# Seventeen unread matrix products in three pauses of TensorE, in a six-stage convolution and attention kernel

## The chip, the core and the metric

The kernel runs on one core of one Trainium2 chip. The metric is the device time of one launch in microseconds (us), the median of several runs. The core's engines are TensorE (PE in the profile, its weight loads PEld), VectorE (DVE), ScalarE (ACT), GpSimd (POOL) and SyncE (SP, which here only issues DMAs). TensorE's clock has two levels, 1.2 and 2.4 GHz; the profile gives the granted clock as a share of the full one, so 0.50 is 1.2 GHz and 1.00 is 2.4 GHz.

## What is computed

Eight images of 64 channels and 16 x 16 pixels pass six residual layers, all in float32:

```python
x = x + _L0_conv_ref(_gn(x), ...)    # group norm, then a deformable 3x3 convolution
x = x + _L1_conv_ref(_gn(x), ...)    # group norm, 3x3 convolution mixed by gates and a 20-step Sinkhorn
t = _to_tokens(x)                    # 8 x 256 tokens of 64 channels
t = t + _L2_attn_ref(_ln_t(t), ...)  # causal attention, 8 heads
t = t + _L2_ffn_ref(_ln_t(t), ...)   # 8 experts, hidden 256, gelu, top 2
t = t + _L3_attn_ref(_ln_t(t), ...)  # windowed gated mean
t = t + _L3_ffn_ref(_ln_t(t), ...)   # 16 experts, hidden 128, silu gate, top 2
```

The three places that the change touches lie in the first group norm, in the Sinkhorn iteration of the second layer, and in the first layer norm ahead of the attention:

```python
def sinkhorn_knopp(H_tilde, t_max=20):
    M = jnp.exp(H_tilde)
    for _ in range(t_max):
        M = M / jnp.sum(M, axis=-1, keepdims=True)
        M = M / jnp.sum(M, axis=-2, keepdims=True)
    return M
```

## The kernel before, in words

Everything is written out by hand. Each engine has one program, executed in order, and the engines meet in counting semaphores: a producer counts one up, a consumer waits for a number. There is no scheduler, so the order in the text of an engine's program is its order on the chip. Channels lie on the partitions for the convolutions (two images side by side, 4 columns of image pairs, `J` = 4), tokens for the attention and the experts. PSUM is one tensor `PS` of 8 banks of 512 float32 columns, and each use names its bank.

TensorE's program in order, with the lines that matter here:

- **First group norm.** VectorE takes the moments of the input. TensorE averages them over pairs of channels by one small product (L1315, bank 7) and sends them back. VectorE and ScalarE make the normalised images (`G`, L798), split them and the offset weights into a high and a low part (`GHP`, L609; `WO`, L612 and L816; `GLP`, L811), and TensorE begins the offset convolution (L1324), which waits for `wo_ready` and for `GHP`: 36 products of 512 columns, in four groups of nine. Then come the offset transposes (L1331) and the products for the taps (L1351).
- **Deformable convolution.** VectorE multiplies the interpolation "hats" (L887), TensorE transposes them (L1379) and applies them (L1363).
- **Second layer.** VectorE and TensorE exchange small products for the group norm and the gate logits (L1391, L1393, L1405). VectorE then runs the Sinkhorn iteration on 8 partitions (L930, L932, L934, 40 half steps of three instructions). Beside it TensorE runs `conv(0)` and `conv(1)` (L1400, banks 1 and 2, float32 products of 512 columns, each two records in the trace) and the products of the attention weights (L1416, L1421); ScalarE scales the convolutions (`scaled_conv_ready`), and GpSimd adds them and makes the remainder `AVL` (L481). When VectorE has the trace of the Sinkhorn matrix (`v3_diag_ready`), TensorE spreads it over the partitions (L1425, bank 0), and VectorE adds the second residual (L947).
- **Entry of the attention stage.** `transpose_x(0)` (L1442, bank 7) gives the tokens, VectorE and GpSimd do the layer norm (L953 to L994), `transpose_y("yA", 0)` (L1452, bank 7) transposes its result, VectorE evacuates it (L998), and the first projections follow (L1465 for queries, L1469 for values; copies on ScalarE L698, L700, remainders on VectorE L1019), with banks 7 and 2 in turn. Then `transpose_x(1)` and the loop over 64 steps of scores (L1524), masks (L1125, L1127), exponentials (L721), transposes (L1536) and value products (L1551 to L1553).
- **Experts.** First the 8-expert layer (L1600, L1619), then the 16-expert layer (L1651, L1636), with the work of the next layer's norms and gates filled in at step numbers written out by hand. The last product is a transpose (L1496), and the output leaves by DMA.

Of the kernel before, what the change touches and what calls it, by code (L numbers as in the profile page):

```python
# [16 lines left out]
P = 128  # L17
J = B // 2
# [139 lines left out]
def hybrid_kernel(nc, x, w64, wcv, wat, w128, wexp, rows, b2, consts, out):  # L158
    with ExitStack() as ctx:
        def sem(name):  # L160
            return ctx.enter_context(nc.semaphore(name))
# [4 lines left out]
        PS = ctx.enter_context(nc.psum_tensor("PS", [P, 8, 512], F32))  # L166


        def sb(name, *shape, dtype=F32):
            return tensor(ctx, name, *shape, dtype=dtype)  # L170

        cst = sb("cst", NCONST)
# [85 lines left out]
        def c_(name):  # L258
            return cst[:, CONST[name]]
# [8 lines left out]
        ident = c_("ident")  # L268
# [65 lines left out]
        scaled_conv_ready = sem("scaled_conv_ready")  # L334
# [423 lines left out]
        def _(dve):  # L758
# [252 lines left out]
            def query_remainders(name):  # L1011
                _, a, i = name
                queries[0] += 1
                if on_side(name):
                    dve.wait_ge(side_filled, SIDE[name] + 1)
                else:
                    dve.wait_ge(misc_filled, FILL[name] + 1)
                dve.wait_ge(qh_copied, queries[0])
                nc.vector.tensor_tensor(QL[:, a % 2, 2 * i:2 * i + 2, :].rearrange("p g n -> p (g n)"), PS[:, 2 if on_side(name) else 7, :],  # L1019
                                        QH[:, a % 2, 2 * i:2 * i + 2, :].rearrange("p g n -> p (g n)").bitcast(F32),  # L1020
                                        ALU.subtract).then_inc(side_free if on_side(name) else misc_free, 1)
# [31 lines left out]
            def first_max(src, m, hot, E):  # L1053

                _, key, _, _, _, _, _, mk, _ = top_views(E)
                step(nc.vector.tensor_reduce(m, src, AX.X, ALU.max))
                settle()
                step(nc.vector.tensor_tensor(key, src, wide(m, E), ALU.is_equal))
                settle()
                step(nc.vector.tensor_tensor(key, key, c_("desc")[:, E3 - E:E3].unsqueeze(1).to_broadcast([P, CHUNK, E]), ALU.mult))  # L1060
                settle()
                step(nc.vector.tensor_reduce(mk, key, AX.X, ALU.max))
                settle()
                step(nc.vector.tensor_tensor(hot, key, wide(mk, E), ALU.is_equal))
                settle()

            def top_first(name, c, E):
                lg, _, h1, _, _, m1, _, _, _ = top_views(E)
                dve.wait_ge(misc_free, FILL[name, c] + 1)
                first_max(lg, m1, h1, E)  # L1070
# [239 lines left out]
        def _(pe):  # L1310
            mm = nc.tensor.matmul

            pe.wait_ge(const_loaded, 16)
            pe.wait_ge(moments_ready, 1)
            mm(PS[:, 7, 0:2 * J], c_("pair_mean"), mv[:, 0].rearrange("p j m -> p (j m)"), start=True, stop=True).then_inc(group_moments_ready, 1)  # L1315


            pe.wait_ge(wo_ready, 2)
            for r in range(2):
                for part, ready, image in ((0, ghp_ready, GHP), (1, glp_ready, GLP)):  # L1320
                    pe.wait_ge(ready, 2 * r + 2)
                    for k in range(TAPS):
                        ky, kx = divmod(k, 3)
                        ins = mm(PS[0:4 * NOFF, 5 + r, :], WO[:, k, :], image[:, 2 * r:2 * r + 2, ky:ky + HH, kx:kx + WW],  # L1324
                                 start=(part + k == 0), stop=(part == 1 and k == TAPS - 1))
# [12 lines left out]
            for ip in range(NP):  # L1338
                j, pt = divmod(ip, PT)
                for h in range(2):  # L1340
# [8 lines left out]
                    for r, (gg, ww) in enumerate(((GH, DH), (GH, DL), (GL, DH))):  # L1349
                        for a in range(2):  # L1350
                            ins = mm(PS[:, 1 + 2 * (n % 3) + a, 0:288], gg[hs, j, px], ww[hs, a * 288:(a + 1) * 288],  # L1351
                                     start=(r == 0), stop=(r == 2))
# [65 lines left out]
            for g in range(HEADS):  # L1418
# [2 lines left out]
                ins = mm(PS[:, 6 + odd, hp * C:(hp + 1) * C], wa[hs, WAT["v"]][:, hp * P:(hp + 1) * P],  # L1421
                         wa[hs, WAT["p"]][:, hp * C:(hp + 1) * C], start=True, stop=True)
            ins.then_inc(av_ready, 1)
            pe.wait_ge(v3_diag_ready, 1)
            mm(PS[:, 0, 0:J], spread, V3[0:B, :, 0], start=True, stop=True).then_inc(cb_ready, 1)  # L1425

# [2 lines left out]
            def take(*name):  # L1429

                assert FILLS[fills[0]] == name, (FILLS[fills[0]], name)
                if fills[0]:
                    pe.wait_ge(misc_free, fills[0])
                else:
                    pe.wait_ge(avh_ready, 4)
                fills[0] += 1

            def transpose_x(j):
                pe.wait_ge(x2_ready, j + 1)
                take("xT", j)  # L1440
                for pt in range(PT):
                    ins = nc.tensor.transpose(PS[:, 7, pt * P:(pt + 1) * P], X1[:, j, pt * P:(pt + 1) * P], ident)  # L1442
                ins.then_inc(misc_filled, 1)
# [3 lines left out]
            def transpose_y(name, c):  # L1447
                yts[0] += 1
                pe.wait_ge(y2_ready, yts[0])
                take(name, c)  # L1450
                for q in range(CHUNK):
                    ins = nc.tensor.transpose(PS[:, 7, q * P:(q + 1) * P], Y2[:, 4 * c + q, :], ident)  # L1452
                ins.then_inc(misc_filled, 1)
# [44 lines left out]


            transpose_x(0)  # L1500
            transpose_y("yA", 0)
            pe.wait_ge(avl_ready, 1)
            pe.wait_ge(misc_free, FILL["yA", 0] + 1)
# [88 lines left out]
            for n in range(N2 + 2):  # L1592
# [9 lines left out]
                if n >= 2:  # L1602
# [6 lines left out]
                    if v % (2 * UNIT) == 0:  # L1609
                        for i in range(2):  # L1610
                            if u >= 2:
# [4 lines left out]
                               start=True, stop=False, skip_group_check=True)  # L1616
# [23 lines left out]
            for n in range(N3 + 2):  # L1640
                if n < N3:
# [3 lines left out]
                    for a in range(2):  # L1645
# [4 lines left out]
                        for k, w in enumerate((WH, WL)):  # L1650
                            ins = mm(PS[:, (2 * n + a) % 3, :], w[:, 1 + a, e * P:(e + 1) * P], YTs[:, c * CW:(c + 1) * CW],  # L1651
                                     start=(k == 0), stop=(k == 1))
# [63 lines left out]
```

## Time and profile before

| | |
|---|---|
| median of 3 runs | 523.0 us (522.67 to 523.0) |
| time of the profiled execution | 523.0 us |
| its span, first to last instruction | 521.2 us |
| mean granted TensorE clock | 0.965 |
| TensorE matmuls busy | 464.2 us, 89% of the span |
| VectorE busy | 361.1 us, 69% |
| ScalarE busy | 266.6 us, 51% |
| GpSimd busy | 170.7 us, 33% |

A busy share is a mean over stages with different limits. The profile cuts the span into 40 slices and gives the busy tenths of each engine and the granted clock in each; "the chain that ended last" follows the last instruction back, at each step to what released it. Idle time of an engine is put down to the instruction that ended it.

### The profile page before, as it was taken

How to read it: one execution, taken by the hardware profiler on the slowest of the kernel's cores; microseconds unless marked ns; L12 is line 12 of the kernel's file. 1: busy time of each engine (PE TensorE's matmuls, PEld its weight loads, DVE VectorE, ACT ScalarE, POOL GpSimd, SP SyncE). 2: the span in 40 equal slices, each digit the busy share in tenths (PEclk: the TensorE clock that was granted, in tenths of full speed). 3: DMA queues.
4: the chain of work that ended last, by engine and by line, in shares of the span. 5: the costliest groups of instructions: out<-in, count | busy, mean ns of one | idle time of the engine just before them, and what ended most of it. 6: DMA issues, size and time to landing. Idle time of an engine off the chain costs nothing.

```text
span 521.2 us, 9463 instructions
## 1 busy us (share of the span) xinstructions
PE 464.2 (89%) x3372; PEld 403.1 (77%) x3372; DVE 361.1 (69%) x1050; ACT 266.6 (51%) x631; POOL 170.7 (33%) x217
## 2 busy tenths in 40 slices
PE   0998999959239999999999999999999989989994
PEld 0687777734228898899999899999999878878893
DVE  3288778358866768978787634266477898787844
ACT  2468666521308897888897544444443223322230
POOL 4800000001312584572233324133263435434332
PEclk9999999979758999999999999999999999999997
DMA  8200000000120303000000000000000000000000
GB/s 201 95 2 1 2 1 1 0 1 1 33 48 3 80 3 82 1 3 1 2 2 1 2 0 2 1 1 0 3 1 0 1 3 0 1 14 8 2 11 10
DMA packets 5458, 8.14 MB, mean 16 GB/s; under 512 B 2850, under 2 KB 4514, under 8 KB 4900
## 3 DMA queue, kind: packets, MB, share of 16 engines
q1 hardware_dynamic: 5268, 7.43, 5.8%
q8 instruction: 27, 0.44, 0.4%
q10 hardware_dynamic: 144, 0.11, 0.1%
q14 instruction: 19, 0.16, 0.1%
HBM read 7.01 MB, written 0.52 MB: 14 GB/s over the span
## 4 chain that ended last, share of the span: by engine, by line
PE 69%; DVE 20%; ACT 4%; issue 4%; DMA 1%; POOL 0%; SPq 0%; DVEq 0%; ACTq 0%; POOLq 0%
PE PS L1651 10%; PE PS L1619 10%; PE PS L1636 9%; PE PS L1363 6%; PE PS L1600 6%; PE PS L1379 6%; PE PS L1524 4%; PE PS L1536 3%; PE PS L1324 2%; DVE M L934 2%; PE PS L1465 2%; PE PS L1553 2%; PE PS L1552 2%; ACT score_arena L721 2%; PE PS L1469 2%
## 5 line engine op out<-in xcount | busy, mean ns | idle before, releaser
L513 POOL TENSOR_TENSOR pr<-pr 128x512 f32<-128x512 f32 (+2 forms) x70 | 67.2, 960 | 108.6 <-DVE pr L1032 37.1
L753 ACT ACTIVATE VV<-PS 128x512 f32<-128x512 f32 x64 | 38.2, 597 | 86.8 <-PE PS L1651 86.8
L1619 PEld LDWEIGHTS PS<-wk,hid 128*128 128x128 f32 x512 | 66.6, 191 | 6.4 <-ACT hid L743 1.2
L1636 PEld LDWEIGHTS PS<-wk,hid 128*128 128x128 f32 x512 | 67.0, 191 | 5.7
L743 ACT ACTIVATE hid<-PS,wk 128x512 f32<-128x512 f32 x64 | 43.8, 687 | 49.2 <-PE PS L1600 49.2
L1619 PE MATMUL PS<-wk,hid 128*128 128x64 f32 x512 | 63.9, 268 | 0.7 <-ACT hid L743 0.7
L1636 PE MATMUL PS<-wk,hid 128*128 128x64 f32 x512 | 64.1, 268 | 0.0
L721 ACT ACTIVATE score_arena<-score_arena,nmx 128x128 f32<-128x128 f32 (+1 forms) x128 | 56.9, 447 | 13.7 <-DVE nmx L1127 13.2
L1258 DVE TENSOR_TENSOR hid<-VV,PS 128x512 f32<-128x512 f32 x64 | 43.8, 686 | 23.2 <-PE PS L1651 16.6
L1651 PE MATMUL PS<-YTs,WH 128*128 128x512 f32 x128 | 57.6, 450 | 1.8 <-DVE hid L1258 1.8
L1651 PE MATMUL PS<-YTs,WL 128*128 128x512 f32 x128 | 50.6, 395 | 0.0
L662 ACT ACTIVATE st_mem<-PS 128x512 f32<-128x512 f32 x72 | 36.5, 614 | 21.6 <-PE PS L1379 21.6
L887 DVE TENSOR_TENSOR prod<-hats 128x768 f32<-128x768 f32 x48 | 42.5, 951 | 0.1
L1524 PE MATMUL PS<-YTs,QH 128*128 128x128 f32 (+1 forms) x128 | 38.3, 323 | 0.0
L1536 PE MATMUL PS<-cst,score_arena 128*128 128x128 f32 x192 | 33.0, 280 | 4.4 <-ACT score_arena L721 3.9
L1379 PEld LDWEIGHTS PS<-cst,prod 128*128 128x128 f32 x288 | 31.3, 141 | 7.1 <-issue 3.5
L1379 PE MATMUL PS<-cst,prod 128*128 128x128 f32 x288 | 34.1, 275 | 2.8 <-DVE prod L887 1.9
L1168 DVE TENSOR_TENSOR pr<-PS,gate 128x512 f32<-128x512 f32 x48 | 30.8, 684 | 7.6 <-PE PS L1619 6.4
L1524 PE MATMUL PS<-YTs,QL 128*128 128x128 f32 (+1 forms) x128 | 36.1, 282 | 0.0
L490 POOL TENSOR_TENSOR lnst<-lnst,cst 128x4 f32<-128x4 f32 x16 | 16.3, 1022 | 56.4 <-DVE lnst L977 56.4
L1363 PE MATMUL PS<-st_mem,U 128*64 128x256 f32 x288 | 33.5, 383 | 0.0
L1019 DVE TENSOR_TENSOR QL<-PS,QH 128x512 fp32r<-128x512 f32 x32 | 22.1, 689 | 14.4 <-ACT QH L698 14.4
(223 smaller groups left out, 1049.4 us busy)
## 6 DMA issues: line engine op xcount, KB each, us to landing
stage<-in_wexp SPq DMA_DIRECT2D x6, 512.0 KB, 5.9
wk<-in_w SPq DMA_DIRECT2D x1, 1032.0 KB, 8.1
wa<-in_wat SPq DMA_DIRECT2D x1, 768.0 KB, 6.3
cst<-in_consts SPq DMA_DIRECT2D x1, 580.0 KB, 6.4
X<-in_x SPq DMA_DIRECT2D x2, 256.0 KB, 5.1
out<-X SPq DMA_DIRECT2D x16, 32.0 KB, 1.9
wc<-in_w SPq DMA_DIRECT2D x2, 183.5 KB, 6.0
score_arena<-in_wcv SPq DMA_DIRECT2D x2, 144.0 KB, 6.1
```

What stands on the lines that cost most here:

```text
L513: step(nc.gpsimd.tensor_tensor(buf[:, :, 0:width], buf[:, :, 0:width], buf[:, :, width:2 * width], ALU.add))
L721: ins = nc.scalar.activation(PR[:, s % 3, cols], MS[:, s % 3, cols], ACT.Exp, bias=nmx[:, s % 3, qt:qt + 1], scale=-1.0, accum_out=rsum[:, ...
L743: nc.scalar.activation(hid[:, n % 3], PS[:, n % 3, :], ACT.Gelu, bias=wk[:, W128["b1"]][:, e2:e2 + 1]).then_inc(gelu_done, 1)
L887: nc.vector.tensor_tensor(prods[unit % 2][:, b].rearrange("p k (a b) -> p k a b", a=HH), hk[:, 0].unsqueeze(3).to_broadcast([P, TRIPLE, HH ...
L1258: nc.vector.tensor_tensor(hid[:, n % 3], sil[:, n % 2], PS[:, (2 * n + 1) % 3, :], ALU.mult).then_inc(prod3_done, 1)
L1363: ins = mm(PS[h * C:(h + 1) * C, 5 + j % 2, 0:S], U[:, 4 * j + 2 * qt + h, k * C:(k + 1) * C], ST[:, v % ST_TAPS, h, qt], start=(k + qt == ...
L1379: ins = nc.tensor.transpose(PS[:, T_BANKS[m % 6], (2 * qt + pt) * P:(2 * qt + pt + 1) * P], prods[i // TRIPLE % 2][:, 2 * pt + h, k % TRIP ...
L1524: ins = mm(PS[:, s % 2, cols], w[:, a % 2, g, qt * P:(qt + 1) * P], YTs[:, a * S:a * S + (qt + 1) * P], start=(r == 0), stop=(r == 1))
L1536: ins = nc.tensor.transpose(PS[:, 3 + v % 2, k * P:(k + 1) * P], PR[:, v % 3, k * P:(k + 1) * P], ident)
L1619: ins = mm(accumulator(u, q, e % UNIT), hid[:, v % 3, q * P:(q + 1) * P], wk[:, W128["w2_2"]][:, r * C:(r + 1) * C], start=False, stop=(v ...
L1636: ins = mm(accumulator(u, q, e % UNIT), hid[:, v % 3, q * P:(q + 1) * P], wk[:, W128["w3"]][:, e * C:(e + 1) * C], start=True, stop=True)
L1651: ins = mm(PS[:, (2 * n + a) % 3, :], w[:, 1 + a, e * P:(e + 1) * P], YTs[:, c * CW:(c + 1) * CW], start=(k == 0), stop=(k == 1))
```

## The change

TensorE's program gets a helper that issues a float32 product of the identity with the first columns of the constants, into a bank that holds nothing live at that time; nothing reads the result. It is called in three places: 4 products of 256 columns into bank 1 behind the first moments product (L1315), 8 products of 512 columns into bank 2 behind the products of the attention weights (L1421), and 5 products of 512 columns into bank 2 between `transpose_x(0)` and `transpose_y("yA", 0)`. Ahead of the second call stands a new wait, for ScalarE to have read the convolution out of bank 2 (`scaled_conv_ready`). Nothing else differs.

```diff
+            def keep_awake(bank, times, width):
+
+                for _ in range(times):
+                    mm(PS[:, bank, 0:width], ident, cst[:, 0:width], start=True, stop=True)
+
             pe.wait_ge(const_loaded, 16)
             pe.wait_ge(moments_ready, 1)
             mm(PS[:, 7, 0:2 * J], c_("pair_mean"), mv[:, 0].rearrange("p j m -> p (j m)"), start=True, stop=True).then_inc(group_moments_ready, 1)
-
+            keep_awake(1, 4, 2 * P)
...
             ins.then_inc(av_ready, 1)
+            pe.wait_ge(scaled_conv_ready, J)
+            keep_awake(2, 8, 4 * P)
             pe.wait_ge(v3_diag_ready, 1)
             mm(PS[:, 0, 0:J], spread, V3[0:B, :, 0], start=True, stop=True).then_inc(cb_ready, 1)
...
             transpose_x(0)
+            keep_awake(2, 5, 4 * P)
             transpose_y("yA", 0)
```

## Rows read from the trace of the kernel before

**Rows 1.** The page: busy time and share by engine, and the granted clock in 40 slices.
```profile
PE 464.2 (89%) x3372; PEld 403.1 (77%) x3372; DVE 361.1 (69%) x1050; ACT 266.6 (51%) x631; POOL 170.7 (33%) x217
PEclk9999999979758999999999999999999999999997
```
**Rows 2.** Chain that ended last, 0 to 30 us: start us, us, what.
```profile
12.70 0.93 ACT GHP L609 x3
13.63 11.01 PE PS L1324 x36
24.63 1.78 PE PS L1331 x16
```
**Rows 3.** Timeline of PE at the start, then windows (us, PE busy, clock, DMA, GB/s).
```profile
9.22 0.57 PE L1315 MATMUL PS<-mv,cst 128*128 128x8 f32 x2 [9.22 <-DVE mv L780]
...
13.62:17.52 3.90, 3.90 (x10) 1.00 0.61 254
17.52:19.84 2.32, 2.32 (x11) 1.00 0.00 0
```
**Rows 4.** Windows of 1 us: busy PE, PEld, DVE, ACT, POOL, then clock.
```profile
109.00:110.00 1.00, 0.00 (x0) 0.00 (x0) 0.63 (x5) 0.20 (x1) 0.00 (x0) 0.77 0.00 0
116.00:117.00 1.00, 1.00 (x3) 0.52 (x2) 0.83 (x5) 0.30 (x2) 0.43 (x3) 0.81 0.00 0
136.00:137.00 1.00, 0.00 (x0) 0.00 (x0) 0.82 (x5) 0.67 (x2) 0.25 (x1) 0.93 0.00 0
160.00:161.00 1.00, 0.83 (x6) 0.54 (x5) 0.39 (x4) 1.00 (x5) 0.00 (x0) 0.63 0.00 0
```
**Rows 5.** Timeline of PE, 98 to 165 us: start us, us, what, idle before.
```profile
101.11 5.40 PE L1363 MATMUL PS<-st_mem,U 128*64 128x256 f32 x48
108.46 0.36 PE L1391 MATMUL PS<-mv,cst 128*128 128x8 f32 x2 [1.95 <-DVE mv L780]
...
132.50 1.22 PE L1421 MATMUL PS<-wa 64*128 64x64 f32 x13
143.01 0.58 PE L1425 MATMUL PS<-V,cst 8*128 8x4 f32 x2 [9.30 <-DVE V L939]
144.38 0.69 PE L1442 MATMUL PS<-cst,X 128*128 128x128 f32 x2 [0.78 <-DVE X L947]
150.67 1.12 PE L1452 MATMUL PS<-cst,Y 128*128 128x128 f32 x4 [5.60 <-DVE Y L994]
```
**Rows 6.** Windows over PE alone, columns as in rows 3: the second layer's convolution.
```profile
113.36:116.36 3.00, 3.00 (x4) 0.50 0.02 5
...
123.08:131.01 7.93, 7.93 (x20) 1.00 0.00 0
```
**Rows 7.** Timeline of DVE: the Sinkhorn iteration and its end.
```profile
137.22 2.98 DVE L934 TENSOR_TENSOR M<-M,mn 8x16 f32<-8x16 f32 x1
...
142.81 0.15 DVE L939 SCALAR_TENSOR_TENSOR V<-V,cst 8x4 f32<-8x4 f32 x1
```
**Rows 8.** Chain that ended last, 143 to 160 us.
```profile
152.66 1.21 PE PS L1465 x4
153.89 0.61 ACT QH L698
154.59 0.70 DVE QL L1019
155.33 2.08 PE PS L1469 x4
157.41 0.59 PE PS L1442 x2
159.68 0.99 ACT score_arena L721 x4
```
**Rows 9.** PE instructions by line, 170 to 285 us: ns min/median/max, first and last start.
```profile
L1452 PE MATMUL PS<-cst,Y x24: 271/273/279, 175.5 to 281.8; 128*128 128x128 f32 x24
...
L1442 PE MATMUL PS<-cst,X x4: 273/276/279, 189.1 to 207.8; 128*128 128x128 f32 x4
...
L1469 PE MATMUL PS<-AVL,YTs x14: 392/397/398, 172.0 to 267.7; 128*128 128x512 f32 x14
...
L1465 PE MATMUL PS<-YTs,AVL x50: 276/279/284, 170.0 to 263.7; 128*128 128x256 f32 x50
```
**Rows 10.** Timeline of ACT: the copies of values and the table load.
```profile
157.45 0.60 ACT L700 ACTIVATE VV<-PS 128x512 f32<-128x512 f32 x1 [0.26 <-PE PS L1469]
158.06 1.28 ACT L721 ACT_TABLE_LOAD   x1
```

## The prediction

> **What bounds the kernel now.** I read the page first. TensorE is busy for 89% of the span, and its granted clock is full in most slices and short of it in a stretch around the second layer [rows 1]. So the products bound most of the kernel, and a product costs twice as much where the clock is at 1.2 GHz. Only stretches where TensorE both works at the low clock and sets the end can give something back; I looked for these with the windows of 1 us. The clock falls at about 109.6 (the slice from 109 shows 0.77, that is 0.54 us at 1.00 and the rest at 0.50), rises at about 116.4, falls at about 136.9, and rises at about 160.7 [rows 4]. Both falls come 3.1 us after the last dense products: the taps end at 106.51, the weight products at 133.72 [rows 5].
>
> The start hides a fourth stretch. The clock column says 1.00 there, but the durations say otherwise: the window from 13.62 holds nine products of the offset convolution in 3.90 us (433 ns each, the tenth record in its count only begins or ends there), and the next nine take 2.32 us (258 ns) [rows 3]. Those are the two levels, so the clock is low from the start to about 17.4. This stretch is on the chain: 36 products in one piece from 13.63, then the transposes [rows 2].
>
> So there are three low stretches of interest. At the start, 3.8 us of chained products run low. From 109.6 to 116.4 the low clock meets small products and the first 3 us of a convolution that runs beside the Sinkhorn iteration. VectorE ends that iteration only at 142.96 [rows 7], 9.3 us after TensorE ran out of work [rows 5], so the convolution is off the path. From 136.9 to 160.7 everything on TensorE is low, and from 143.01 on most of it is in the chain [rows 5, 8].
>
> **Part by part: the first pause.** Four float32 products of 256 columns are added behind L1315, which ends at 9.79 [rows 3]. The nearest rows for one are those of the convolution: four records, two products of 512 columns, begin in 3.00 us at low clock; eighteen records take 7.93 us at high clock, 0.88 us per product [rows 6]. Twice that, 1.76, is the low price (records 0.88 us apart, of which four begin in 3.00 us), so 256 columns cost 0.88 low. Four cost 3.5 us: 9.7 to 13.2. The first real product begins at 13.62, because `GHP` and `WO` are ready then [rows 2], so they are covered with 0.4 us to spare; if each were 10% dearer, they would still be covered. What they buy: the two rises after unbroken work came 3.0 us (113.36 to 116.4) and 3.8 us (13.62 to 17.4) behind its beginning [rows 3, 4, 6]. From 9.7 that is 12.7 to 13.5, so the nine products find the high clock, or meet it after the first. Eight by 175 ns is 1.4 us; bounds 0 (no rise before 17.4) and 1.6 (all nine). TensorE is never starved in the 36, so the gain reaches the end of the transposes, and all later work shifts.
>
> **The small products from 106.5 on.** They shift with the rest; whether the clock falls before or behind L1393 is worth 0.2 us. I take 0. The convolution behind them may run low for up to 1.4 us longer, which costs TensorE 0.7 us. The cover is the 9.3 us in front of L1425.
>
> **The second pause.** The new wait is for ScalarE's four scalings, which follow `conv(1)`; TensorE still has L1416 and L1421 to do then, so I price it at nothing. Behind it stand only the eight unread products and L1425. At the high clock eight cost 8 x 0.88 = 7.0 us: 133.7 to 140.8, and L1425 starts at 143.01 [rows 5, 6]. That leaves 2.2 us, or 1.5 if the low convolution took 0.7. VectorE is held for 2.98 us in one step of the iteration at 137.22 [rows 7]; nothing here makes that shorter. The gain: with the last dense work at 140.8 instead of 133.7, the fall comes 3.1 us later, at 143.9 instead of 136.9. L1425 runs high, 0.36 as L1391 did instead of 0.58: 0.2 us [rows 5]. The two transposes of L1442 take 0.69 low and, from single ones of 0.276 spaced by half the low spacing, 0.38 high [rows 5, 9]: 0.3 us; they lie on the fall, so I take half, 0.15.
>
> **The third pause.** Five products follow from 144.9, and L1452 waits for the layer norm until 150.67 [rows 5]: 5.7 us of cover. At the high clock they cost 5 x 0.88 = 4.4 us and are hidden. At the low one they cost 5 x 1.76 = 8.8 us, end at 153.7 and hold the transposes, all projections and the whole attention loop for 3.0 us. I expect between: the clock falls just ahead of them and rises again 3.0 to 3.8 us into them. In 3.4 low us 1.9 products are done, the other 3.1 take 2.7 us: end at 151.0, a delay of 0.3 us. Then the clock is high for what was low:
>
> - four transposes, 1.12 us low; high 3 x 0.107 + 0.273 = 0.59 [rows 5, 9]: 0.5 us;
> - four query products, 1.21 low; high 3 x 0.12 + 0.28 and a start of 0.05 = 0.7 [rows 8, 9]: 0.5 us;
> - from the first query remainder (done 155.29) to the first exponential (159.68) 4.4 us pass [rows 8]. High, the second query's copy no longer waits for TensorE; value products cost 0.22 apiece instead of 0.43. The first value bank is full 0.75 us behind the remainder, the second 1.4; two copies of 0.60 end 2.0 behind it, and the table load of 1.28 [rows 10] ends at 3.3. ScalarE, with its table load, now sets this: 1.1 us gained, bounds 0.5 and 1.4.
>
> Of the transposes the Trainium skill (TensorE: Matmul & The Clock Gate, Part 4: PE-mode transpose) says that the full clock does not engage for them. By that page the 0.5 us of the four transposes would be missing and the time would be about 519.9. The trace disagrees: the same line takes 273 ns in the high stretch, against 435 in the low one [rows 5, 9].
>
> **The sum.** 1.4 + 0.2 + 0.15 + 0.5 + 0.5 + 1.1 - 0.3 = 3.55 us. The profiled execution took 523.0 us (span 521.2), equal to the median of the runs, so the forecast is 519.4 us. Behind 161 us the clock was high before as well, and the attention loop inherits the shift.
>
> **The rivals.** A difference under 0.2% (1.0 us) is what a measurement of this kernel can't tell from no change.
>
> 1. *The first pause buys nothing.* The engine pauses 0.4 us between the unread products and the real ones. For: the rise at 160.7 came 8.0 us behind 152.66, in a stretch with short pauses, so pauses can put it off [rows 4, 8]. Against: the pause here is a tenth of the stretch. Time 519.4 + 1.4 = 520.8.
> 2. *The clock doesn't hold through the entry of attention.* After the third call TensorE waits for VectorE's evacuations, and half of the time stands idle even if warm. If the clock falls or never rises there, only the first pause and L1425 pay: 523.0 - 1.6, with up to 0.3 of delay: 521.5. For: the low clock held over that very stretch before. Against: no fall is seen behind less than 3 us with nearly no work.
> 3. *The third call is too long.* The clock falls at 143.9 and rises late, so its five products end at up to 153.7: +3.0 in place of +0.3, and the rest as forecast: 519.4 + 2.7 = 522.1. It would need a rise more than 5 us into unbroken work, where 3.0 and 3.8 were seen.
> 4. *Unread products don't hold the clock (slower).* The moving operand is mostly zeros. If such products count for nothing, the clock falls at 136.9 in the middle of the second call: 3.2 us high do 3.6 products, the other 4.4 cost 7.7 us, end 144.6, and L1425 is 1.6 us late; the third call costs 3.0 us. The first pays nothing. Time 523.0 + 4.6 = 527.6. What decides is whether the clock is still 1.00 past 137. For: no row shows such products. Against: the float32 convolution, same form, lifted the clock [rows 4, 6].
> 5. *The point of the rise is chance.* If the rise comes at another point in each run, the gain of the first pause lies anywhere from 0 to 1.6 us and the delay in the third from 0 to 0.3, which moves the time between 518.9 and 520.8, inside the range. Against: the three times before lie within 0.33 us, where such a draw would have moved them by more than 1 us. The Trainium skill (same page, Part 1) does state this: the number of low products at a start differs from run to run. By that page the runs before should have spread; they don't.
>
> **How the numbers follow.** Forecast, with its own range 518.3 to 520.3: 0.52. Rival 1: 0.16. Rival 2: 0.11. Rival 3: 0.07. Rival 4: 0.05. Rival 5: 0.06. Something unseen, such as no gain passing the attention loop: 0.03. Faster than 521.95: the forecast, rivals 1 and 5, and nine tenths of rival 2, with a third of rival 3: 0.86, which I lower to 0.83. Within 0.2%: 0.10. Slower: 0.07. The range reaches from every upper bound at once (1.6 + 0.2 + 0.3 + 0.5 + 0.5 + 1.4, and 0.2 for L1393: 4.7 us, 518.3, less 0.2 for the spread of the runs) to rival 3: 518.1 to 522.1.
>
> **What would show it.** The first nine records of L1324 at 258 ns apart, or 433; the start of L1331 at 23.2, or 24.5. The clock at 1.00 from 137 to beyond 143. The five products from 143.5: their end against the end of VectorE's L994. L1465 records of 0.28 us instead of 0.41. The first exponential 3.5 us earlier than 159.68. Wrong would be: a fall inside the second call, unread products that end behind L994 by more than 1 us, or an attention loop that takes longer by what it was given.

## The result, and the profile after

The changed kernel takes 520.44 us (median of 20 runs, 518.99 to 524.85), the kernel before 523.57 us (20 runs, 522.67 to 525.58). The ratio is 0.9948, with a 95% interval of 0.9929 to 0.9966: 2.7 us faster (1.8 to 3.7); the two medians differ by 3.1. Single times of the changed kernel spread over 5.9 us, and the five of its twenty above 523 have a lower mean granted clock (0.975 to 0.977) than the other fifteen (0.979 to 0.987). The profiled execution took 519.7 us, 3.3 us less than the one of before, with a span of 517.9 and a mean clock of 0.980. The forecast was 519.4, range 518.1 to 522.1.

The page after: busy time, and the granted clock in 40 slices, against [rows 1].

```profile
PE 476.3 (92%) x3406; PEld 408.0 (79%) x3406; DVE 360.5 (70%) x1050; ACT 266.5 (51%) x631; POOL 170.8 (33%) x217
PEclk9999999979979999999999999999999999999997
```

TensorE is busier by 12.1 us, though the kernel is shorter: the three calls take 3.43 + 7.13 + 6.05 = 16.6 us by the rows below, and the real products less than before. Thirty-four records were added, two for each of the 17 products.

The timeline of PE after, at the start (start us, us, line, what, idle before), against [rows 3]:

```profile
9.62 0.57 PE L1320 MATMUL PS<-mv,cst 128*128 128x8 f32 x2 [9.62 <-DVE mv L780]
10.04 3.43 PE L1316 MATMUL PS<-cst 128*128 128x256 f32 x8
14.02 2.56 PE L1329 MATMUL PS<-GHP,WO 128*108 128x512 f32 x9 [0.55 <-ACT GHP L609]
16.42 2.48 PE L1329 MATMUL PS<-GLP,WO 128*108 128x512 f32 x9
...
23.37 1.95 PE L1336 MATMUL PS<-cst,OT 108*128 108x54 f32 x16
```

L1316 is the helper's product; the lines of TensorE's program stand 5 to 8 higher than before, so L1324 is L1329 here, L1425 is L1432, L1452 is L1459. Everything begins 0.4 us later than before (9.62 against 9.22), because the input arrived later (VectorE's first instruction waits for it until 7.26, before until 6.86). The first nine products now begin 16.42 - 14.02 = 2.40 us ahead of the next nine, where it was 3.90, and the next nine take 2.31: nearly all of the first nine ran at the high clock. The 36 take 9.35 us.

The timeline of PE after, from the second call on, against [rows 5]:

```profile
132.61 7.13 PE L1316 MATMUL PS<-cst 128*128 128x512 f32 x16
141.39 0.38 PE L1432 MATMUL PS<-V,cst 8*128 8x4 f32 x2 [1.65 <-DVE V L939]
142.55 0.58 PE L1449 MATMUL PS<-cst,X 128*128 128x128 f32 x2 [0.78 <-DVE X L947]
142.92 6.05 PE L1316 MATMUL PS<-cst 128*128 128x512 f32 x10
148.81 0.60 PE L1459 MATMUL PS<-cst,Y 128*128 128x128 f32 x4
```

The second call ends 1.65 us before L1432 is released, so it is covered. The third runs from 142.92 to 148.8 and ends 0.1 us behind L994, whose last row is `148.25 0.42` on VectorE. The windows of 1 us give the clock (busy PE, PEld, DVE, ACT, POOL, then clock):

```profile
141.00:142.00 1.00, 0.38 (x2) 0.29 (x2) 0.47 (x3) 0.00 (x0) 0.00 (x0) 1.00 0.55 180
142.00:143.00 1.00, 0.45 (x3) 0.45 (x4) 0.48 (x1) 0.00 (x0) 0.00 (x0) 0.86 1.18 262
...
146.00:147.00 1.00, 1.00 (x3) 0.38 (x2) 0.87 (x4) 0.00 (x0) 1.00 (x2) 0.94 0.00 0
...
152.00:153.00 1.00, 0.54 (x2) 0.30 (x2) 1.00 (x2) 0.10 (x1) 0.00 (x0) 0.98 0.00 0
...
156.00:157.00 1.00, 0.94 (x6) 0.73 (x5) 0.91 (x7) 0.79 (x4) 0.00 (x0) 0.82 0.00 0
```

Read a partial value as the share of the microsecond at the high level. The clock falls at 142.7, just ahead of the third call, is back at 146.1, and is low once more from 153.0 to 156.4. Ahead of that second fall TensorE had paused twice for copies of the first projections, 0.87 us before 150.28 and 1.03 us before 152.46. The chain of after through the entry of attention, against [rows 8]:

```profile
150.28 0.71 PE PS L1472 x4
151.02 0.61 ACT QH L698
...
151.72 0.70 DVE QL L1019
...
152.46 1.82 PE PS L1476 x4
154.28 0.45 PE PS L1449 x2
...
156.42 0.98 ACT score_arena L721 x4
```

The query products take 0.71 us instead of 1.21. The value products (L1476) take 1.82, little less than the 2.08 of before, since the clock fell in the middle of them. From the first exponential (3.26 us earlier than before) to the end nothing is given back: the last gain is 3.3.

### The profile page after: what moved, and what is told of

It reads as the page before. It is cut to its first block, busy times and chain, and to the rows that moved or that the text cites. A ratio compares the mean times of both kernels' runs of the same rounds, so it can differ in the third digit from the quotient of the medians.

```text
span 517.9 us, 9531 instructions
## 1 busy us (share of the span) xinstructions
PE 476.3 (92%) x3406; PEld 408.0 (79%) x3406; DVE 360.5 (70%) x1050; ACT 266.5 (51%) x631; POOL 170.8 (33%) x217
## 4 chain that ended last, share of the span: by engine, by line
PE 70%; DVE 20%; ACT 4%; issue 4%; DMA 1%; SPq 0%; DVEq 0%; ACTq 0%
PE PS L1659 11%; PE PS L1627 10%; PE PS L1644 9%; PE PS L1368 6%; PE PS L1608 6%; PE PS L1384 6%; PE PS L1532 4%; PE PS L1544 3%; DVE M L934 2%; PE PS L1329 2%; PE PS L1560 2%; PE PS L1561 2%; PE PS L1472 2%; ACT score_arena L721 2%; PE PS L1476 1%
## 5 line engine op out<-in xcount | busy, mean ns | idle before, releaser
L490 POOL TENSOR_TENSOR lnst<-lnst,cst 128x4 f32<-128x4 f32 x16 | 16.3, 1022 | 55.5 <-DVE lnst L977 55.3
```

## The experiments

Each run is timed against the kernel before on its own chip. The diffs are against the changed kernel unless said otherwise.

| run | median us | lowest, highest (runs) | before us | ratio, 95% interval |
|---|---|---|---|---|
| p1_only | 522.85 | 521.26, 525.66 (12) | 524.23 | 0.9968 (0.9950 to 0.9987) |
| p2_only | 524.07 | 522.77, 527.51 (12) | 524.23 | 1.0008 (0.9983 to 1.0033) |
| p3_only | 523.10 | 521.81, 524.08 (12) | 524.23 | 0.9980 (0.9964 to 0.9996) |
| p12 | 523.37 | 521.02, 524.97 (12) | 524.23 | 0.9976 (0.9956 to 0.9997) |
| after_again | 520.26 | 518.80, 524.15 (12) | 523.63 | 0.9944 (0.9923 to 0.9965) |
| guard_yd | 520.72 | 520.13, 525.70 (12) | 523.63 | 0.9966 (0.9941 to 0.9991) |
| third_3 | 521.67 | 518.91, 525.08 (12) | 523.63 | 0.9966 (0.9944 to 0.9988) |
| filled | 522.47 | 520.20, 524.25 (12) | 523.63 | 0.9970 (0.9950 to 0.9990) |
| guard_yc | 520.43 | 519.91, 522.19 (6) | 523.84 | 0.9936 (0.9917 to 0.9955) |
| before_yc | 523.57 | 522.94, 524.26 (12) | 523.84 | 0.9993 (0.9982 to 1.0004) |
| filled_yc | 519.34 | 519.00, 520.25 (6) | 523.84 | 0.9915 (0.9896 to 0.9934) |
| bridge_yc | 520.37 | 518.91, 522.20 (6) | 523.84 | 0.9933 (0.9911 to 0.9954) |

And what the profiled execution of each shows in us: the 36 products of the offset convolution, from their start to that of L1331's; from the start of L1425 to the first transpose of the attention loop (L1536); and where the clock was low inside the experts. Line names are those of the kernel before.

| profile | 36 products | L1425 to L1536 | low in the experts |
|---|---|---|---|
| before | 10.9 | 17.7 | no |
| p2_only | 11.8 | 17.2 | no |
| p3_only | 10.7 | 16.9 | no |
| before_yc | 11.7 | 17.7 | no |
| p1_only | 10.0 | 17.7 | no |
| p12 | 10.0 | 17.3 | 424.9 to 428.3 |
| after | 9.4 | 16.1 | no |
| after_again | 9.4 | 15.4 | no |
| guard_yd | 9.4 | 15.4 | 422.8 to 426.2 |
| third_3 | 9.4 | 16.8 | 423.7 to 427.1 |
| guard_yc | 9.8 | 16.3 | no |
| filled | 10.0 | 15.3 | 422.1 to 428.9 |
| filled_yc | 9.4 | 15.3 | no |
| bridge_yc | 10.1 | 15.2 | no |

Three more readings of the fourteen profiles: the first product of TensorE starts between 8.98 and 10.04 us, with the arrival of the input (VectorE begins on it between 6.62 and 7.68), which moves the time by up to 1.1 us. From the first hidden product of the 8-expert layer (L1600) to the last of the 16-expert layer (L1651) 225.1 to 225.2 us pass in the ten profiles without a low clock there, 226.7 in p12 and third_3, 227.9 in guard_yd and 229.4 in filled. And in after_again and guard_yd the clock was low for 3.4 us in the first layer too, from 37.4 and 37.1, behind a pause of 0.9 us, while TensorE ran transposes (L1379); it cost nothing, since VectorE sets the pace there (84.0 us from L1331 to L1391 with it and without).

### One call at a time: p1_only, p2_only, p3_only, p12

```diff
 p1_only: the first call alone
-            pe.wait_ge(scaled_conv_ready, J)
-            keep_awake(2, 8, 4 * P)
-            keep_awake(2, 5, 4 * P)
 p2_only: the second call and its wait alone
-            keep_awake(1, 4, 2 * P)
-            keep_awake(2, 5, 4 * P)
 p3_only: the third call alone
-            keep_awake(1, 4, 2 * P)
-            pe.wait_ge(scaled_conv_ready, J)
-            keep_awake(2, 8, 4 * P)
 p12: the first and second call
-            keep_awake(2, 5, 4 * P)
```

> Keeps only the first call (4 products of 256 columns behind the first moments product). Theory: the gains add up, so this gives 1.4 us at L1324 (36 products in 9.5 us instead of 11.0), and the time is 522.2 where the kernel before has 523.6. Rival (the clock comes at another point in each run): the profiled run may show the 36 products at 9.5 or 11.0 us, and the times spread over about 1.5 us. Rival (most of the 3.1 us of the change comes from here, by the shifted Sinkhorn as well): 521.5.

> Keeps only the second call (8 products of 512 columns behind the weight products). Theory: the clock is still high when L1425 and perhaps L1442 run, 0.2 to 0.5 us gained, then it falls before the projections, which run low as before: 523.2, same as before within the measurement. Rival (a high clock at the entry of attention lasts by itself): the projections run high, up to 2 us gained, 521.5.

> Keeps only the third call (5 products of 512 columns between the first transposes of the attention stage and the transposes of the normalised tokens). The clock has fallen 6 us before them. Theory: they start low, the clock rises within 3 to 3.8 us, they end up to 0.5 us late, and the transposes and first projections run high: 1.5 us gained, 522.0. Rival (a late rise): they end up to 3 us behind L994 and hold the attention loop, no gain or 1 us lost, 523.6 to 524.6, in some of the runs or in all.

> Keeps the first and the second call. Theory (gains add): 1.4 + 0.4, 521.8; the whole change has 520.4. Rival (the third call is what makes the slow draws of 523 us and more among the runs of the change): no time of this kernel is above 523, while its median is no worse than the change's. If the slow draws come from the first pause, they stay.

The first call alone gives 0.32% (1.7 us, interval 0.7 to 2.6), in line with the 1.4 of the theory. The timeline of PE in p1_only:

```profile
9.40 3.76 PE L1316 MATMUL PS<-cst 128*128 128x256 f32 x8
13.38 3.23 PE L1329 MATMUL PS<-GHP,WO 128*108 128x512 f32 x9 [0.22 <-ACT GHP L609]
16.44 2.48 PE L1329 MATMUL PS<-GLP,WO 128*108 128x512 f32 x9
```

Here the nine begin 3.06 us ahead of the next nine, between the 3.90 of a low clock and the 2.40 of after: the rise came in the middle of them. So the pause's gain is a draw, and the rival that said so is right on that point. Over all profiles the 36 take 9.4 to 10.1 us with the call (ten profiles) and 10.7 to 11.8 without (four). The two don't overlap: the call gave in every profile, 1.6 us between the means.

The second call alone gives nothing that can be measured, as forecast. The timeline of p2_only shows why: the small product and the transposes run high, the four transposes of yA low again.

```profile
144.19 0.38 PE L1431 MATMUL PS<-V,cst 8*128 8x4 f32 x2 [1.05 <-DVE V L939]
145.35 0.44 PE L1448 MATMUL PS<-cst,X 128*128 128x128 f32 x2 [0.78 <-DVE X L947]
151.40 1.11 PE L1458 MATMUL PS<-cst,Y 128*128 128x128 f32 x4 [5.61 <-DVE Y L994]
```

The third call alone gives 0.2% (1.0 us, interval 0.2 to 1.9; 1.5 had been expected). Its timeline is the late rise of the third rival, in one draw:

```profile
144.59 7.22 PE L1316 MATMUL PS<-cst 128*128 128x512 f32 x10
151.65 0.60 PE L1456 MATMUL PS<-cst,Y 128*128 128x128 f32 x4
```

L994 was done at 150.35 (start 149.92, 0.43 us), so the transposes stood 1.3 us behind unread work, which had run low until 150.1. That is a rise 5.5 us into unbroken work, and real products can wait as long: in p2_only the first nine of the offset convolution took 3.97 us and the next nine 3.21, with records 0.43 us apart up to 20.43, so the rise came some 6 us behind their start at 14.32. Behind it all projections ran high, so that 16.9 us remained of 17.7.

p12 was expected at 521.8 if the gains add. It gave 0.24% (1.3 us, interval 0.2 to 2.3), no more than the first call alone, and seven of its twelve times lie above 523. So the third call isn't what makes such times. The five from 524.2 up have a mean granted clock of 0.967 to 0.970, the other seven 0.973 to 0.975: more low clock goes with them, but where it lay no run shows. The profiled execution is one of the seven (0.973), and it has a low stretch too. It took 523.1 us, as long as the one before, though it reached the attention loop 1.4 us earlier. The timeline of PE in p12, late in the 16-expert stage, shows the reason (L1658 is the product of the hidden layers, L1459 the transposes of a layer norm):

```profile
423.33 0.66 PE L1459 MATMUL PS<-cst,Y 128*128 128x128 f32 x4 [1.50 <-DVE Y L994]
423.93 0.50 PE L1658 MATMUL PS<-YTs,WH 128*128 128x512 f32 x1
424.27 0.40 PE L1658 MATMUL PS<-YTs,WL 128*128 128x512 f32 x1
424.50 1.44 PE L1643 MATMUL PS<-wk,hid 128*128 128x64 f32 x8
425.70 0.77 PE L1658 MATMUL PS<-YTs,WH 128*128 128x512 f32 x1
426.28 0.63 PE L1658 MATMUL PS<-YTs,WL 128*128 128x512 f32 x1
```

TensorE waited 1.5 us for VectorE's L994, and 1.6 us after that, in dense work, the clock fell: records of 0.40 us become 0.63. The stretch costs 351.7 us from the attention loop to the last hidden product, against 349.8 in after; 1.6 of the 1.9 us lie inside the experts. The same pause of 1.5 us is in the kernel before, ahead of its L1452 at 424.52, so such a fall may be open to all of these kernels.

### The same kernel again, and a first guard: after_again, guard_yd

after_again has no edit. guard_yd:

```diff
                 yts[0] += 1
-                pe.wait_ge(y2_ready, yts[0])
-                take(name, c)
+                if (name, c) == ("yD", 2):
+                    take(name, c)
+                    keep_awake(7, 3, 2 * P)
+                    pe.wait_ge(y2_ready, yts[0])
+                else:
+                    pe.wait_ge(y2_ready, yts[0])
+                    take(name, c)
```

> The changed kernel itself, unchanged, as the yardstick for its three neighbours in this group and as a second profiled execution. Theory (the points at which the clock falls and rises differ from run to run): the profile shows other points than 142.7, 146.1, 153.0 and 156.4, the 36 products of L1329 take 9.5 us or up to 11, the median is 520.4 to 522, and single times reach 523 to 525. Rival (the points are tied to the program): the same points as in the first profile, within 0.3 us.

> The changed kernel, with three more unread products of 256 columns in the pause of 1.5 us that TensorE has in the 16-expert stage ahead of the transposes of yD 2. In the profile of p12 the clock fell 1.5 us behind that pause for 3.4 us and cost 1.5 us. Theory (a fall there in some runs makes part of the slow times): no profile shows a low clock between 300 and 500 us, the highest time is at least 1 us lower than that of the changed kernel, and the median 0 to 0.7 us lower. Rival (that fall was a stray event, or the slow times come from the entry of attention alone): spread and median as the changed kernel's.

after_again repeats the result (0.9944). In its profile the clock falls at 143.2, is back at 146.6 and doesn't fall again in the entry, so the value products run high. Its chain:

```profile
152.62 0.74 PE PS L1476 x2
153.38 0.60 ACT VV L700
153.99 0.60 ACT VV L700
154.61 1.28 ACT L721
155.90 0.98 ACT score_arena L721 x4
```

From the first remainder (152.58) to the first exponential 3.3 us pass, which is what the prediction had worked out for a clock that holds, and the chain is on ScalarE with its table load. In after, where it didn't hold, 4.0 pass. The points are thus not tied to the program. The 36 products took 9.4 us both times, so this pair shows nothing of a draw at the start.

guard_yd rests on a mistake of mine: the pause isn't ahead of yD 2, it is ahead of yC 3. Its profile shows the pause untouched (1.49 us) and a fall at 422.8. The three products stand ahead of yD 2 instead, where TensorE has no pause, and real work waits for them:

```profile
432.37 0.40 PE L1664 MATMUL PS<-YTs,WL 128*128 128x512 f32 x1
432.61 1.46 PE L1316 MATMUL PS<-cst 128*128 128x256 f32 x6
433.90 0.60 PE L1464 MATMUL PS<-cst,Y 128*128 128x128 f32 x4
```

From 432.61 to 433.90 they take 1.3 us, in the place where after goes straight from one to the other. That is the difference between the 227.9 us of its experts and the 226.7 of p12 and third_3, which have a fall of the same length. So guard_yd is no test of the theory. It shows what an unread product costs where there is no pause: its full price.

### The third call shorter, and every pause filled: third_3, filled

```diff
 third_3
-            keep_awake(2, 5, 4 * P)
+            keep_awake(2, 3, 4 * P)
 filled
             keep_awake(1, 4, 2 * P)
+            keep_awake(1, 1, P)
...
-            keep_awake(2, 8, 4 * P)
+            keep_awake(2, 9, 4 * P)
             pe.wait_ge(v3_diag_ready, 1)
             mm(PS[:, 0, 0:J], spread, V3[0:B, :, 0], start=True, stop=True).then_inc(cb_ready, 1)
+            keep_awake(2, 1, 2 * P)
...
             transpose_y("yA", 0)
+            keep_awake(0, 1, 2 * P)
...
             for name in FIRST_PROJECTIONS:
                 project(name)
+                if name == FIRST_PROJECTIONS[1]:
+                    keep_awake(0, 1, 4 * P)
 and the guard ahead of yD 2, as above
```

> The third call with 3 products instead of 5. Theory: three end before L994 even at the low clock (5.3 us of 5.7), so nothing can be late, but where the clock has fallen it may not rise before the projections, which then run low. In runs without a fall nothing changes. Median 0.5 us above the changed kernel's, highest time no higher. Rival (five products delay more than they give): median below the changed kernel's by 0.3 us or more.

> The changed kernel with every pause of its three places filled further: one more product of 128 columns in the first call, nine instead of eight in the second, one of 256 columns behind L1432, one of 256 behind the four transposes of yA 0, one of 512 behind the first two query projections, and the guard ahead of yD 2. Theory: with no pause of TensorE over 0.9 us between the convolution and the attention loop, the clock stays high from there on in every run; L1476 and L1532 run high as well (another 0.5 to 1 us); the median is 519.0 to 519.7 and the times lie within 2 us. Rival (the added products are in the way of projections that are ready): the entry of attention is 0.5 us longer, no gain over the changed kernel.

The profile of third_3 is the case that its theory feared. Three products end at 147.8, TensorE then waits 1.3 us, the clock falls at 150.6, and the projections run low:

```profile
143.37 4.44 PE L1316 MATMUL PS<-cst 128*128 128x512 f32 x6
149.13 0.66 PE L1459 MATMUL PS<-cst,Y 128*128 128x128 f32 x4 [1.32 <-DVE Y L994]
150.66 0.55 PE L1472 MATMUL PS<-YTs,AVH 128*128 128x256 f32 x1 [0.88 <-DVE YTs L998]
```

Its median is 1.4 us above after_again's, where 0.5 had been expected, and its highest time is 0.9 us higher, where no higher one had been expected. The intervals overlap, so this is a direction rather than a size: five are not too many. That the last two carry the clock over is likely where the call is entered at the low clock. Where it is entered at the high one, five end early as well: in guard_yc they leave the same pause of 1.3 us, and the clock fell at 151.6 for 6.8 us; in bridge_yc they leave it too, and the clock held.

filled held the clock high from 118.3 to 422.1, and the entry took 15.3 us. But its profiled execution took 229.4 us in the experts instead of 225.1. The clock fell there for 6.8 us behind the same pause ahead of yC 3, and the misplaced guard took 1.3 us of its own, as it does in every execution. The prediction of its run failed (522.47 where 519.0 to 519.7 was expected). The misplaced guard accounts for 1.3 us of that; falls in the experts are the likely rest, for the mean clock of the twelve runs is 0.982 to 0.988, against 0.985 to 0.990 for filled_yc below, which differs only in the guard's place.

### The guard in its place: guard_yc, before_yc, filled_yc, bridge_yc

The guard is the same diff with `("yC", 3)`. before_yc is the kernel before with the helper and this guard alone. filled_yc is filled with this guard in place of the other. bridge_yc is the changed kernel with the guard, nine products in the second call, and one of 256 columns behind L1432, without the products in the waits of the projections.

> The changed kernel with three more unread products of 256 columns where the pause really is: ahead of the transposes of yC 3 in the 16-expert stage (the run guard_yd had them ahead of yD 2, in a place without a pause, and the clock still fell at 422.8). Theory (this pause of 1.5 us makes part of the slow times, with a different draw in each run): the pause shrinks to about 0.2 us, no low clock between 300 and 500 us, no time above 522.5, median 519.9 to 520.3. Rival (the slow times come from elsewhere): spread as the changed kernel's, with times above 523.

> The kernel before with only this guard (three unread products of 256 columns ahead of the transposes of yC 3, none of the three calls of the change). Theory (the late fall strikes both kernels alike): the slow times of the kernel before go as well: none above 525, median 522.7 to 523.2 against 523.6 to 524.2. Rival (only the changed kernel is open to it): no difference from the kernel before.

> The kernel filled (every pause of the three places filled further) with the guard moved to yC 3. Its profile had the clock high from 118.3 to 422.1, and a fall there of 6.8 us. Theory: no fall from the convolution of the second layer to the end, median 519.0 to 519.8, all times within 2 us. Rival (the products behind the transposes and behind the first queries are in the way of real ones): above the changed kernel with the guard by 0.3 us or more.

> The changed kernel with nine products instead of eight in the second call, one of 256 columns behind L1432, and the guard at yC 3, but nothing in the waits of the projections. Theory: the third call is always entered at the high clock, so it never ends late, median 519.4 to 519.9 and no time above 521.5. Rival (the third call's late ends cost nothing that matters): no difference from the changed kernel with the guard alone.

The timeline of PE in guard_yc shows the pause filled; 0.2 us is left of 1.5:

```profile
420.34 1.46 PE L1316 MATMUL PS<-cst 128*128 128x256 f32 x6
422.00 0.66 PE L1464 MATMUL PS<-cst,Y 128*128 128x128 f32 x4 [0.20 <-DVE Y L994]
```

guard_yc was expected at 519.9 to 520.3 with no time above 522.5; it has 520.43 and 522.19, and its ratio (0.9936) can't be told from the changed kernel's (0.9948, 0.9944). No run of the four with this guard has a time above 524.3, and none of their four profiles shows a low clock in the experts, where four of the ten others did (p12, guard_yd, third_3, filled). Four profiles without one could still be chance at that rate (about one in five).

For before_yc a median of 522.7 to 523.2 and no time above 525 had been expected. The median didn't move (523.57, ratio 0.9993), and though its highest time is 524.26, where the kernel before has 525.68 beside it, that 525.68 came with a clock of 0.966, as high as any of the seventeen there, so nothing points to a low stretch in it. In the other two groups the kernel before has 70 times, and its four highest (526.7 to 527.9) have the lowest clock of all, 0.961 against 0.962 to 0.966 for all others but one. By this a further low stretch strikes the kernel before as well, in few of its runs. Where it lies is not shown, since the one profile of that kernel caught none, and neither is it shown that the guard removes it there.

filled_yc takes 519.34 us, all six times within 1.3 us, ratio 0.9915 (0.9896 to 0.9934). Its clock rises at 116.1 and stays at 1.00 until 512.1, behind the last expert's products, which end at 509.2. The entry of its profile:

```profile
148.81 0.66 PE L1466 MATMUL PS<-cst,Y 128*128 128x128 f32 x4 [1.31 <-DVE Y L994]
149.31 0.60 PE L1316 MATMUL PS<-cst 128*128 128x256 f32 x2
150.35 0.35 PE L1479 MATMUL PS<-YTs,AVH 128*128 128x256 f32 x1 [0.44 <-DVE YTs L998]
151.37 1.02 PE L1316 MATMUL PS<-cst 128*128 128x512 f32 x2
152.54 0.50 PE L1483 MATMUL PS<-AVH,YTs 128*128 128x512 f32 x1 [0.15 <-DVE QL L1019]
```

The added products leave 0.44 and 0.15 us before real ones, so they are in nobody's way. By the ratio it is 4.5 us faster than the kernel before (3.5 to 5.4); against the changed kernel the intervals of the ratios just touch (0.9934 and 0.9929). bridge_yc (520.37, up to 522.20) missed what was expected of it (519.4 to 519.9, none above 521.5): it can't be told from guard_yc (520.43), though its profile shows the third call entered at the high clock and the clock held. With six runs each, the 1.0 us between it and filled_yc isn't settled.

## Why the prediction was right

**The first pause.** Forecast: the four products are covered, and 1.4 us are gained (bounds 0 and 1.6). Measured in the profiled execution: end at 13.5, 0.55 us before the real work, and 11.01 us of chained products [rows 2] became 9.51: 1.5 us. p1_only gives 1.7 by its median. Right. The first rival, that the 0.4 us without work would spoil it, is wrong in all eight profiles that have this pause (0.2 to 0.55 us; filled and filled_yc close it). Of all ten profiles with the call, five gained 0.4 to 0.8 us less than after.

**The small products and the convolution.** Forecast 0 and no cost. In the profile the shift between L1329 and L1432 grew from -1.1 (23.53 against 24.63) to -1.6 us. The 0.5 us isn't the clock's: a step of the Sinkhorn iteration that took 0.7 us in before, beside GpSimd's additions (L478), has no counterpart in after, where only one step took 0.45 (0.46 in before). How VectorE's steps fall beside GpSimd's differs from execution to execution, and I didn't test it further.

**The second pause.** Forecast: covered, the fall moved to 143.9, L1425 0.2 us and L1442 0.15 us shorter. Measured: covered by 1.65 us, the fall at 142.7, L1432 at 0.38 instead of 0.58, L1449 at 0.58 instead of 0.69. By itself it gives nothing (p2_only). Its use seems to lie in the third pause, which it hands a clock that fell late: in their profiles p3_only was held up by 1.3 us, after by 0.1.

**The third pause.** Forecast: entered at about the fall, a rise 3 to 3.8 us later, end 0.3 us late. Measured: fall at 142.7, rise 3.2 us into the call, end 0.1 us late in after. The four transposes gave 0.5 and the four query products 0.5, as worked out. The Trainium skill (TensorE: Matmul & The Clock Gate, Part 4: PE-mode transpose) says that transposes don't get the full clock; the changed kernel doesn't bear that out either: L1459's four take 0.60 us at the high clock where four took 1.12 at the low one.

**The stretch to the first exponential.** Forecast 1.1 us (bounds 0.5 and 1.4), measured 0.4 in the profiled execution: this is the term that was mis-sized there, by the second fall at 153.0. Rival 2 had named such a loss of the clock, at 0.11. In after_again, without that fall, it measures 1.1. So the number was right for a clock that holds and was taken for certain where it is one of two outcomes.

**The sum.** 1.50 - 0.40 (late input) + 0.52 (Sinkhorn) + 0.21 + 0.03 (L1449, less the late end) + 0.52 + 0.49 + 0.39 = 3.26 us for the profiled pair. The terms of the clock alone make 3.1 of it; the late input and the Sinkhorn step, neither of them forecast, nearly cancel, which is luck. The medians of 20 runs differ by 3.1 us and the ratio gives 2.7 (1.8 to 3.7), where 3.55 had been forecast.

**What I had wrong.** Rival 5 got 6%, on the evidence that three times of the kernel before lay within 0.33 us. Twenty times lie within 2.9 us, thirty-five on another chip within 5.6. Three runs were no evidence. The Trainium skill (TensorE: Matmul & The Clock Gate, Part 1) says that the start of the high clock varies from run to run, and the profiles agree: 9.4 to 10.1 us with the call, 10.7 to 11.8 without. The forecast held because most draws give most of the gain. And the sentence that no fall is seen behind less than 3 us with nearly no work held for the one trace I had; a fall came behind 1.5 us in p12 and behind 0.9 in after_again.

Rival 4 (unread products of mostly zeros don't hold the clock) is refuted by every profile with a second call: 1.00 from the convolution to beyond its end. The first 512 columns of the constants, which these products read, are zero in some three quarters of their places, the first 256 in 99 of 100 (counted in the kernel's `shape_constants`). Rival 3 happened in p3_only, in part, and rival 2, a clock that doesn't hold through the entry, happened in after for the value products and in third_3 for all projections.

## What to carry to other kernels

A pause of TensorE can cost twice: once while it waits, and again when the work behind it runs at 1.2 GHz. Where the profile shows a low clock in a chained stretch, unread products that end before the real ones are ready give back up to half of that stretch; size them for the clock they will find, since they cost up to twice as much at the low one (the five of the third call took 4.46 us at the high clock in guard_yc and 7.22 in p3_only). Make sure of the pause: three products where there was none cost their full 1.3 us in guard_yd. One filled pause may only move the fall to the next, so look at the whole stretch: the second call was worth nothing alone, and filling all the pauses was worth 4.5 us (filled_yc), against 2.7 to 3.4 for the three calls (the change, and guard_yc). And where the time spreads by 1% between runs, look at several profiles and at the mean clock of every run: behind pauses of 0.9 to 1.5 us inside dense work the clock fell in some executions only.

## What the runs showed of the hardware that I hadn't expected

- The granted clock reads 1.00 at the start of each profile, while the durations show the low level until between 13 and 20 us (20.4 in p2_only). The first products of every profile that has no call ahead of them run low.
- One pause of 1.5 us in dense work was followed by a low clock for 3.4 us (p12, guard_yd, third_3) or 6.8 us (filled), and in other executions by nothing (after, after_again). A pause of 0.9 us was followed by 3.4 us of it in two of fourteen profiles (after_again, guard_yd).
- Products with the identity against mostly zeros held the clock at 1.00 (second call, 7.1 us) and raised it: with the first call the first nine products of the offset convolution take 2.40 to 3.17 us, without it 3.77 to 3.97.
- A VectorE multiply of 8x16 elements took 2.97 us (after) and 2.98 us (before) instead of 0.17, beside a GpSimd subtraction of 128x1536 elements that took 3.4 us.
